# Second attention of a decoder layer: a tile's transposes moved from TensorE to DMA, and work moved ahead within the step

## The reference

```python
x = x + self_attention(layernorm(x))           # over the 4 rows, 16 heads of 32
x = x + cross_attention(layernorm(x), ctx)     # 2048 queries, 128 keys, 16 heads of 32
x = x + gate(layernorm(x))
# cross attention
q, k, v = x @ Wq.T + bq, ctx @ Wk.T + bk, ctx @ Wv.T + bv
scores = q k^T / sqrt(32);  masked;  attn = softmax(scores)
out = (attn v) @ Wo.T + bo
# gate: 64 inputs s, each through 16 hinges
s = x @ Win + bin_;  h = relu(s[..., None] * W1 + b1)
g = sum_h(h * W2) + b2;  out = g @ Wout + bout
```

## Time and profile before

| | |
|---|---|
| median of 3 runs | 1730.53 us (1727.5 to 1731.91) |
| the profiled execution | 1728.16 us, span 1726.2 us |
| busy share of the span | PE 93%, PEld 77%, DVE 81%, ACT 56%, POOL 68% |
| granted clock of TensorE | 0.979 on the mean |
| transposes by DMA | 160, 10 per step |

### The profile page before, as it was taken

How to read it: one execution, slowest core, us unless ns; L and a number is a source line. 1 busy time by engine, 2 the same in 40 slices (tenths; PEclk the granted TensorE clock), 3 DMA queues, 4 the chain that set the end, 5 groups by cost and what they waited for, 6 DMA issues and landing times.

```text
span 1726.2 us, 35517 instructions
## 1 busy us (share of the span) xinstructions
PE 1614.0 (93%) x13184; PEld 1326.2 (77%) x13184; DVE 1401.6 (81%) x1931; ACT 975.0 (56%) x2316; POOL 1172.5 (68%) x801
## 2 busy tenths in 40 slices
PE   6899999999999999999689999999999999999985
PEld 5678888888888888887577777777777777777774
DVE  6789888888898888877648888788888888888876
ACT  3434444433344444434348777777677787777773
POOL 3276666666677776669378667787667786677850
PEclk9999999999999999999789999999999999999997
DMA  5311111111111011144154444654455644365441
GB/s 215 124 34 47 50 50 49 49 49 49 30 43 49 24 49 49 49 92 76 50 106 77 98 96 113 125 103 111 87 113 113 131 95 106 94 111 123 100 81 55
DMA packets 241741, 140.89 MB, mean 82 GB/s; under 512 B 191168, under 2 KB 199488, under 8 KB 241600
## 3 DMA queue, kind: packets, MB, share of 16 engines
q1 hardware_dynamic: 241024, 138.92, 34.1%
q10 hardware_dynamic: 576, 0.07, 0.0%
HBM read 59.92 MB, written 37.09 MB: 56 GB/s over the span
## 4 chain that ended last, share of the span: by engine, by line
PE 67%; ACT 13%; DVE 9%; issue 6%; POOL 3%; DMA 2%; SPq 0%; ACTq 0%; POOLq 0%; DVEq 0%
PE qb L452 28%; PE ring L1548 12%; PE ob L588 10%; ACT prob_c L1761 7%; PE sc L1576 5%; PE ring L1553 4%; PE tb L460 3%; PE sc L1548 2%; DVE g_sb L1886 2%; PE sc L1568 2%; ACT pT L1727 2%; ACT sc L1740 1%; PE ring L1586 1%; ACT p L1777 1%; DMA w_first<-in_wqkv 1%
## 5 line engine op out<-in xcount | busy, mean ns | idle before, releaser
L452 PE MATMUL qb<-wqkv,xT 128*128 128x512 f32 x2304 | 552.1, 394 | 6.1 <-DVE wqkv L1022 6.1
L452 PEld LDWEIGHTS qb<-wqkv,xT 128*128 128x128 f32 x2304 | 429.8, 189 | 93.8 <-DVE wqkv L1022 6.3
L1761 ACT ACTIVATE prob_c<-sc,ntop 128x128 f32<-128x128 f32 x1024 | 284.2, 391 | 25.9 <-DVE ntop L1913 23.9
L1548 PE MATMUL ring<-wqkv 128*128 128x512 f32 x960 | 253.6, 409 | 28.5 <-DVE wqkv L1895 19.0
L1548 PEld LDWEIGHTS ring<-wqkv 128*128 128x128 f32 x960 | 174.5, 192 | 83.2 <-DVE wqkv L1895 25.5
L357 POOL TENSOR_TENSOR prod_pool<-v,prob 128x1024 f32<-128x1024 f32 x64 | 179.9, 2811 | 64.5 <-DVE prob L917 59.4
L1913 DVE TENSOR_REDUCE ntop<-sc 128x4 f32<-128x512 f32 x256 | 171.5, 681 | 26.5 <-PE sc L1576 26.5
L588 PE MATMUL ob<-wout,aT 128*128 128x512 f32 x768 | 191.5, 398 | 0.8 <-DVE aT L947 0.8
L668 ACT ACTIVATE v<-qb 128x512 f32<-128x512 f32 x64 | 38.3, 598 | 260.1 <-PE qb L452 249.7
L1479 POOL TENSOR_TENSOR p<-prob_c,p 128x1024 f16<-128x1024 f32 x80 | 171.6, 2145 | 16.3 <-ACT p L1777 16.2
L1548 PE MATMUL ring<-xT_c,wqkv 128*128 128x512 f32 x720 | 176.6, 401 | 2.6 <-DVE attn_c L1978 2.6
(11 more groups left out here) (153 smaller groups left out, 3267.5 us busy)
## 6 DMA issues: line engine op xcount, KB each, us to landing
x_tile<-in_x SPq DMA_DIRECT2D x16, 1024.0 KB, 5.5
x_scratch<-xres SPq DMA_DIRECT2D x16, 1024.0 KB, 4.6
x_tile<-x_scratch SPq DMA_DIRECT2D x16, 1024.0 KB, 5.5
out<-x SPq DMA_DIRECT2D x64, 256.0 KB, 2.0
kt<-k_scratch SPq DMA_DIRECT2D x16, 512.0 KB, 3.7
v_c<-v_scratch SPq DMA_DIRECT2D x16, 272.0 KB, 4.4
raw<-in_wqkv SPq DMA_DIRECT2D x3, 1024.0 KB, 8.9
pT<-p SPq DMA_TRANSPOSE x160, 3.2
```

The costliest lines, as they stand in the source:

```text
L452: last = nc.tensor.matmul(qb[g % 4][:, :], xT[p][a][:, k, t * P:(t + 1) * P], wqkv[b][:, k, c * D:(c + 1) * D], start=(n == 0), stop=(n == ...
L1548: last = nc.tensor.matmul(dst, s, m, start=(n == 0), stop=(n == len(terms) - 1))
L1761: last = nc.scalar.activation(prob[:, h, :], sc[g][:, (h % 4) * C:(h % 4 + 1) * C], ACT.Exp, bias=ntop[:, h:h + 1])
```

## The change

- Tile 1's exponentials go by DMA for all heads. `prob_T(4)` and `prob_T(5)` in slot 2 go, with their evacuations. `part_hi(1, 1)` is new on ACT in slot 2 ahead of `attn_hi(2)`, `part_lo(1, 1)` on POOL ahead of `norm2(j, 2)`, and `turn(j, 1, 1)`, two DMAs, on SP ahead of the store of slot 2.
- On PE `norm2_T(0)` goes ahead of `out_proj(0)`, and `norm2_T(2)` (the second block's norm) ahead of `values(2)`.
- `prob_hi(2)` on ACT goes ahead of `exps(1, 0)`, and `prob_lo(3)` on DVE ahead of `tops(1, 2)`.
- The hinges are spread 4, 3, 1, 0 over the four query products, where they were 3, 2, 2, 1, and the gate's parts come at the third, not the fourth. On DVE `normalise(3)` comes after two hinges and not after three.
- The ring's list follows, and a step now takes 36 places and no bank is skipped. Ties that change: attn_T(1) takes the bank of norm2_T(0), norm_T(0) that of norm2_T(2), norm_T(1) one of values(2), values(2) those of attn_T(2) and ffn_out(2).

```diff
@@ -1182,10 +1182,10 @@
 
 def slot_turns(t):
     if t == 0:
-        return [("out", 0), ("aT", 0), ("pv", 0), ("wo", 0), ("x2T", 0), ("pT", 0), ("pT", 1)]
-    late = [("pT", 2 * t), ("pT", 2 * t + 1)]
+        return [("out", 0), ("aT", 0), ("pv", 0), ("x2T", 0), ("wo", 0), ("pT", 0), ("pT", 1)]
+    late = [("pT", 2), ("pT", 3)] if t == 1 else []
     if t < 3:
-        return [("aT", t)] + late + [("out", t), ("wo", t), ("pv", t), ("x2T", t)]
+        return [("aT", t)] + late + [("out", t), ("wo", t)] + [("pv", t), ("x2T", t)][::1 if t == 1 else -1]
     return ([("aT", 3), ("xT", 0), ("out", 3), ("xT", 1), ("wo", 3), ("xT", 2), ("xT", 3), ("pv", 3), ("x2T", 3)]
             + [("q", m) for m in range(DK)])
 
@@ -1198,7 +1198,7 @@
     "aT": lambda j, i: 4 * j + i - 1,
     "wo": lambda j, i: 4 * j + i - 1,
     "x2T": lambda j, i: 4 * j + i - 2,
-    "pT": lambda j, i: 6 * j + i + 1,
+    "pT": lambda j, i: 4 * j + i + 1,
     "xT": lambda j, i: 4 * j + i + 1,
     "q": lambda j, i: 4 * j + i + 1,
     "s": lambda j, i: j,
@@ -1207,7 +1207,7 @@
 
 
 
-HINGE_RUNS = ((0, 3), (3, 2), (5, 2), (7, 1))
+HINGE_RUNS = ((0, 4), (4, 3), (7, 1), (8, 0))
 
 
 def hinge_bank(n):
@@ -1217,12 +1217,12 @@
 
 def quarter(i):
 
-    return divmod(i if i < 4 else i + 2, 4)
-
-
-def parts_over(j, t, part):
-
-    return (3 * j + t - 1, 2 * j + t - 2)[part]
+    return divmod(i, 4)
+
+
+def parts_over(j, t):
+
+    return 3 * j + t - 1
 
 
 def relu_banks(n):
@@ -1410,7 +1410,7 @@
 
             def turn(j, t, part):
 
-                m = parts_over(j, t, part)
+                m = parts_over(j, t)
                 heads = slice(8 * part, 8 * part + 8)
                 for h, made in enumerate((p_hi[part], p_lo[part])):
                     wait(sp, made, m + 1)
@@ -1432,6 +1432,7 @@
                         store(j, p, t)
                     if t == 1 and has(j):
                         turn(j, 1, 0)
+                        turn(j, 1, 1)
                 if has(j):
                     turn(j, 2, 0)
                     turn(j, 2, 1)
@@ -1512,6 +1513,7 @@
                 if has(j, 1):
                     norm(2)
                 part_lo(1, 0)
+                part_lo(1, 1)
                 norm2(j, 2)
                 if has(j, 1):
                     norm(3)
@@ -1622,16 +1624,16 @@
                     pp = (j - (t == 0)) % 2
                     n = over - 1
                     made, tile = divmod(n, 4)
-                    if tile < 2:
-                        wait(pe, taken["pT"], TURNS_OVER["pT"](made, 2 * tile + 3))
+                    if tile == 0:
+                        wait(pe, taken["pT"], TURNS_OVER["pT"](made, 3))
                     if t == 1:
                         pe.wait_ge(v_in[pp], 16 * (j // 2 + 1))
                     bank(j, ("pv", t))
                     dst = value_sums(j, t)
                     for h in range(H):
                         head = head_of(h)
-                        if h % 8 == 0 and tile > (0, 1)[h // 8]:
-                            wait(pe, turned[h // 8], 32 * (parts_over(made, tile, h // 8) + 1))
+                        if h % 8 == 0 and tile > 0:
+                            wait(pe, turned[h // 8], 32 * (parts_over(made, tile) + 1))
                         for i, (a, b) in enumerate(PASSES):
                             last = nc.tensor.matmul(dst[:, head // 8, head % 8, :], pT[n % 2][a][:, h, :],
                                                     v[:, pp, b, head, 0:DH + 1],
@@ -1686,19 +1688,23 @@
                 scores(0)
                 attn_T(0)
                 values(0)
+                norm2_T(0)
                 out_proj(0)
-                norm2_T(0)
                 prob_T(0)
                 prob_T(1)
                 for t in (1, 2):
                     scores(t)
                     attn_T(t)
-                    prob_T(2 * t)
-                    prob_T(2 * t + 1)
+                    if t == 1:
+                        prob_T(2)
+                        prob_T(3)
                     ffn_out(t)
                     out_proj(t)
+                    if t == 2:
+                        norm2_T(t)
                     values(t)
-                    norm2_T(t)
+                    if t == 1:
+                        norm2_T(t)
                 scores(3)
                 attn_T(3)
                 norm_T(0)
@@ -1753,10 +1759,10 @@
                     if not has(j):
                         return
                     wait(act, topped, 16 * j + 4 * t + g + 1)
-                    if t == 1 or (t == 2 and g >= 2):
-                        wait(act, psum["pT"], TURNS_OVER["pT"](j, g if t == 1 else g + 2))
+                    if t == 1:
+                        wait(act, psum["pT"], TURNS_OVER["pT"](j, g))
                     else:
-                        wait(act, p_lo[g // 2], parts_over(j, max(t, 1 + g // 2), g // 2))
+                        wait(act, p_lo[g // 2], parts_over(j, max(t, 1)))
                     for h in range(4 * g, 4 * g + 4):
                         last = nc.scalar.activation(prob[:, h, :], sc[g][:, (h % 4) * C:(h % 4 + 1) * C],
                                                     ACT.Exp, bias=ntop[:, h:h + 1])
@@ -1764,13 +1770,13 @@
 
                 def prob_hi(i):
                     t, g = quarter(i)
-                    if g == 0 or i == 4:
+                    if g == 0:
                         wait(act, psum["pv"], 4 * j + t - 1)
                     take_hi(j, "pT", i, pT[t][0][:, 4 * g:4 * g + 4, :])
 
                 def part_hi(t, part):
 
-                    m = parts_over(j, t, part)
+                    m = parts_over(j, t)
                     heads = slice(8 * part, 8 * part + 8)
                     wait(act, exped, 16 * j + 4 * t + 2 * part + 2)
                     wait(act, turned[part], 32 * m)
@@ -1820,10 +1826,14 @@
                     if t == 1:
                         prob_hi(0)
                         prob_hi(1)
+                    if t == 2:
+                        part_hi(1, 1)
                     attn_hi(t)
+                    if t == 1:
+                        prob_hi(2)
                     exps(t, 0)
-                    prob_hi(2 * t)
-                    prob_hi(2 * t + 1)
+                    if t == 1:
+                        prob_hi(3)
                     exps(t, 1)
                     part_hi(t, 0)
                     exps(t, 2)
@@ -1852,7 +1862,7 @@
                     hinges(*HINGE_RUNS[m])
                     if m == 0:
                         norm2_hi(3)
-                    if m == 3:
+                    if m == 2:
                         gate_hi()
                     if has(j, 1):
                         take_hi(j, "q", m, q[0][:, m, :], ACT.Identity, bias=bq[:, m:m + 1])
@@ -2026,10 +2036,12 @@
                         prob_lo(1)
                     attn_lo(t)
                     tops(t, 1)
-                    prob_lo(2 * t)
+                    if t == 1:
+                        prob_lo(2)
                     add_out(t)
+                    if t == 1:
+                        prob_lo(3)
                     tops(t, 2)
-                    prob_lo(2 * t + 1)
                     tops(t, 3)
                     add_attn(t)
                     normalise(t)
@@ -2057,11 +2069,14 @@
                     nc.vector.scalar_tensor_tensor(out=hinge[:, 1, :], in0=hinge[:, 0, :], scalar=bin_[:, 0:1],
                                                    in1=hinge[:, 1, :], op0=ALU.mult, op1=ALU.add).then_inc(hinge_ready, 1)
                 for m in range(DK):
-                    hinges(*HINGE_RUNS[m])
                     if m == 0:
+                        hinges(0, 2)
                         normalise(3)
+                        hinges(2, 2)
                         norm2_lo(3)
-                    if m == 3:
+                    else:
+                        hinges(*HINGE_RUNS[m])
+                    if m == 2:
                         gate_lo()
                     if has(j, 1):
                         wait(dve, hi["q"], TURNS_OVER["q"](j, m))
```

## The result

The changed kernel takes 1709.9 us (median of 4 runs, 1709.7 to 1711.4), the kernel before 1729.0 beside it; the ratio is 0.9895, 95% interval 0.9876 to 0.9914. By the medians it is 1.1% faster.

The account below looks back on a forecast made before the run. The prediction took slots 1 and 2 as held by a chain through ScalarE, slot 3 and queries by TensorE. Gains of 0.5 us in 14 steps and 0.8 in the last, 7.8 in all, gave 1722 us, range 1713 to 1731.

Parts of the forecast that it names:

- slots 0 and 1: Stretch from scores(0) to scores(2): norm2_T(0) runs in out_proj(0)'s wait, 0.4 us earlier, of which only 0.25 passes.
- slot 2: Stretch from scores(2) to scores(3): without pT transposes and their evacuations it takes 8.77 us instead of 9.32, 0.55 less.
- norm_T(0) on the bank of norm2_T(2): After scores(3): norm_T(0) must wait for norm2_lo(2) to free its bank, which gives back 0.3 us per step.
- late landing, to the second query product: After scores(3): part_hi(3,0) waits for a DMA transpose, ScalarE loses 0.4 to 1.4 us, and the first relus are late.
- normalise(3) two hinges behind: Before the second query product: normalise(3) comes 0.8 us earlier, which would have removed a 0.18 wait; late relus eat that.
- rest of the hinge part, gate: Query products: the gate's 0.81 us wait before ffn_out(0) moves behind it; nothing gained, between 0 and 0.81.
- The step that failed: From scores(3) to the second query product: earlier normalise(3) and late relus cancel, leaving 0.5 us gained, bounds 0.1 and 1.0.
- all of it: Rival: give-backs don't bite, the gate's wait or TensorE's 1.04 counts whole; 1.0 to 1.3 us per step; chance 0.18.
- Slot 1: Stretch from scores(1) to scores(2): VectorE's order makes tops(1,2) end only 0.37 us earlier, so 0.25 of 0.4 passes.
- Slower: Rival: tile 1's low transpose of heads 8 to 15 lands late for values(2); 0.9 us lost per step, 1743; chance 0.08.
- port: Rival: POOL's part_lo(1,1) stretches three VectorE instructions in scores(2)'s stretch, 2.0 us a step if doubled, 1751; chance 0.02.

Follow-up runs that it names:

- c1: Kernel before with norm2_T(0) ahead of out_proj(0) in TensorE's list only, the ring's list unchanged: 1722.8 us.
- b2: Kernel before with only tile 1's heads 8 to 15 moved from TensorE to DMA, all other orders as before: 1727.6 us.
- a4: Changed kernel with hinges, gate and normalise(3) put back as before: 1723.9 us.
- c4: Changed kernel with hinges and gate as before, but normalise(3) still after two hinges: 1711.3 us.
- b1: Kernel before with norm2_T(0) ahead of out_proj(0) in both TensorE's and the ring's list, so it takes attn_T(0)'s bank: 1728.2 us.
- c6: Changed kernel with the evacuations prob_hi(2), prob_lo(2) and prob_lo(3) in their places of before: 1708.5 us.
- a7: Changed kernel with part_lo(2,0) ahead of norm(3) on POOL and norm2_lo(2) ahead of statistics(2) on VectorE: 1705.7 us.
- a6: Changed kernel with norm2_lo(2) ahead of statistics(2) on VectorE: 1710.8 us.
- a8: Changed kernel with values(2) ahead of norm2_T(2) again, and the ring's list with it: 1710.0 us.
- a5: Changed kernel with part_lo(2,0) ahead of norm(3) on POOL: 1707.2 us.

## Why the prediction was wrong

| term, us per step | forecast | measured | by which run |
|---|---|---|---|
| slots 0 and 1 | -0.25 | -0.39 (17.52 to 17.13) | after, c1 |
| slot 2 | -0.55 | -0.54 | after, b2 |
| norm_T(0) on the bank of norm2_T(2) | +0.3 | 0 beside the landing | a4 as b2 |
| late landing, to the second query product | 0 with the next row | +0.61 | b2, a4 |
| normalise(3) two hinges behind | 0 with the row above | -0.84 | c4 against a4 |
| rest of the hinge part, gate | 0 | -0.08 | a4 less c4 |
| sum | -0.5 | -1.24 (1.23 by the steps) | |

**The step that failed** is the one that says normalise(3) "would have taken the 0.18 before the second query product, and the late relus eat that". Two sizes in it were wrong. The wait in the earlier trace rows is 0.33 by the starts of the two products and costs 0.43, not 0.18. And the cost of the late relus and the gain of the earlier normalise(3) were set against each other as if they were equal. The relus make the wait 0.86 (run a4); one hinge less ahead of normalise(3) is 0.9 (VectorE's instructions start at 1249.67 and 1250.58), so the move hides the old wait and the new cost together. The prediction charged 0.3 for the bank and nothing for this pair, which is worth -0.23 (0.61 - 0.84).

Counted along TensorE, the 0.7 per step that the forecast missed is this: 0.43 for the wait before the second query product, which is gone; 0.14 in slots 0 and 1; 0.14 because the bank costs 0.16 (the first query product starts 12.26 after scores(3), 12.10 before) and not 0.3; and 0.05 behind the last query product.

That the landing makes the relus late is read off ScalarE's rows in b2 and a4. No run takes the landing's delay away while normalise(3) stays in its old place.

**Slot 0 and the mechanism of slot 2 held.** The 0.4 is there, and c1 and b1 show that it hangs on the free bank, which the prediction took for granted. Slot 2 was read off the last step of the trace before to 0.01 us, the wait of out_proj(2) is 0.77 against the 0.6 to 0.7 said, and "all of it" (TensorE's 1.04 counting whole) was wrong although its time, 1711 to 1715, is nearest: the product wait ate that, and the rest came from elsewhere.

**Slot 1** was forecast 0.15 longer, from VectorE's order. It is 0.04 longer, and c6 shows the order to be worth nothing. The runs in which attn_T(1) has the bank of norm2_T(0), b1 among them, have 9.37 or 9.38, the others 9.32 to 9.34, so the 0.04 looks like that tie, which the prediction put at nothing, at worst 0.1.

**norm_T(0)** starts 2.58 after scores(3) where it was 2.22, 0.36 against 0.3 forecast. Only 0.16 of it reaches out_proj(3) (4.10 after scores(3), 3.94 before), since that had waited for the attention's low part. In the changed kernel this bank and the landing each hold the rest near 25.4, and only the run that lifts both (a7) reaches 25.22; lifting the bank's wait alone (a6, a8) leaves 25.41 to 25.44, the landing's alone (a5) 25.37.

**The gate**: nothing gained, as forecast. Its wait of 0.81 turned into 0.97 before scores(0) and is worth 0.1 at most. "Slower" and "port" fell: there is no steady wait for the new transposes in values(2), and POOL's copies (96 of them) and VectorE's instructions take 2.14 and 0.68 as before.

**The sum over the kernel.** The profiled spans differ by 16.6 us, where the forecast had 7.8. Steps 2 to 14 give 11.5 (13 x 1.23 = 16.0, less 3.4 for the two long steps, less 1.4 for the five of 51.5 to 51.8, plus 0.3 for the odd step before); step 0 gives 3.4, the last step 0.3, where I had 0.8, and the first block, which is unchanged, 1.7; step 1 is 0.3 longer. The first block's end varies from 842.9 to 845.7 over the runs, so its part is not the change's.

So the step that failed is worth 5.0 us in steps 2 to 14 together with the smaller terms (11.5 against 6.5), and about as much, 5.1, comes from step 0 and the first block, where nothing shows that the change made it. If none of that second part is the change's, the change alone would have given about 1715 (an estimate, 1709.9 + 5.1), inside the range, and that the time fell below the range is luck with the clock and the first block.

## What to carry to other kernels

Where a wait is made longer by one part of a change and shortened by another, take both to the instruction that waits: what is left of the wait is the larger of nothing and their difference, and here two parts that are worth 0 and 0.5 alone were worth 0.85 together (0.54 in slot 2 and 0.31 in the rest). Measure a wait on TensorE by the distance of starts against that of the same two groups without a wait. When the order of work and the order of buffers are one list, a trial that moves one moves the other; keep them apart to find which of them pays.

## What was not expected of the hardware

- The transpose for which part_hi(3,0) waits in the changed kernel, the low part of tile 2's first half, lands 3.2 to 3.7 us after issue in steps 1 to 14, but 4.9 in steps 3 and 9, and those take 53.0 us. Steps of 53 us with the same wait of 2.2 to 2.4 come up in single places: 3 and 6 of a6, 6 of a8. Other transposes of the same trace take 4 to 7 us, mostly at places where nothing waits for them. What delays them isn't shown.
- Granted TensorE clock of one and the same stretch, 876 to 900 us, was from 0.79 to 1.00 over runs of nearly the same program, with step 0 between 59.6 and 55.5 us to match. 0.79 is 2.4 GHz for about 60% of the stretch and 1.2 GHz for the rest. Ahead of it, from 848 to 864 us, both kernels were granted 0.50, while TensorE waited for ScalarE and VectorE four times, 0.9 to 2.6 us each.
